# A two-layer attention kernel's set-up: a table load, the small weight products and the slot clearing change places

## The reference

```
xn = layernorm(x)
s  = softmax(q k^T / sqrt(8) + bias[t - s]) v @ w_out + b_out    # 16 heads of 8
g  = silu(sum over the 2 best of 8 experts: weight * expert(xn))
x  = x + s * g
xn = layernorm(x)
s  = (resid * causal_softmax + skip * I - centre * uniform) v @ cproj_w
g  = silu(xn @ W^T + b + (xn @ V_r) @ C^T)
x  = x + s * g
```

## Time and profile before

| what | us |
| --- | --- |
| median of three runs | 993.75 |
| profiled execution | 994.62 |
| its span, first to last instruction | 992.4 |
| TensorE busy | 844.7 (85%) |
| VectorE busy | 726.2 (73%) |
| ScalarE busy | 454.1 (46%) |
| GpSimd busy | 348.1 (35%) |
| start of the first pass of batch 0 | 53.43 |
| start of VectorE's step 1 | 96.68 |

### The profile page before, as it was taken

The page is one execution under the profiler, slowest core; times in us unless marked ns, Lnnn a source line. Parts: engine busy times, 40 slices in busy tenths (PEclk is TensorE's granted clock), DMA queues, the critical chain, the costliest instruction groups (busy, mean ns, idle before and its releaser), DMA issues.

```text
span 992.4 us, 21521 instructions
## 1 busy us (share of the span) xinstructions
PE 844.7 (85%) x7798; PEld 545.6 (55%) x7813; DVE 726.2 (73%) x1155; ACT 454.1 (46%) x803; POOL 348.1 (35%) x369
## 2 busy tenths in 40 slices
PE   1896999999999999887999995255799899999986
PEld 0563555555555555443666663144566676777763
DVE  7638899999998899985767774753377676776753
ACT  1523455444455454443444443582445445454532
POOL 7001755553111111000444444731233433535332
PEclk9987999999999999997999998577799999999998
DMA  5795444444222223231222223304435345354410
GB/s 141 245 191 103 101 98 102 102 108 100 66 64 64 65 64 80 50 120 35 68 65 66 67 69 92 110 17 97 80 87 115 82 101 107 86 116 90 106 28 11
DMA packets 105540, 88.37 MB, mean 89 GB/s; under 512 B 12565, under 2 KB 97497, under 8 KB 102409
## 3 DMA queue, kind: packets, MB, share of 16 engines
q1 hardware_dynamic: 96780, 76.54, 33.8%
q0 software_dynamic: 4352, 8.99, 3.2%
q10 hardware_dynamic: 4352, 2.10, 0.9%
HBM read 45.69 MB, written 41.11 MB: 87 GB/s over the span
## 4 chain that ended last, share of the span: by engine, by line
PE 20%; issue 14%; POOL 8%; DMA 6%; ACT 3%; DVE 2%; SPq 1%; POOLq 0%; ACTq 0%; DVEq 0%
PE ps L751 7%; POOL probs L1221 5%; DMA ks<-parts_d 3%; PE ps L772 3%; PE ps L763 2%; POOL qkr L1208 2%; POOL qk L1213 2%; ACT rows L967 1%; PE ps L753 1%; DMA parts_d<-qk 1%; PE ps L745 1%; PE ps L1487 1%; PE ps L1555 1%; PE ps L1547 1%; DMA probs<-mixed 1%
## 5 line engine op out<-in xcount | busy, mean ns | idle before, releaser
L1269 DVE TENSOR_REDUCE mx<-ps 128x4 f32<-128x1024 f32 (+1 forms) x224 | 270.1, 1219 | 109.6 <-PE ps L1487 75.2
L1410 ACT ACTIVATE probs<-probs 128x1024 f32<-128x1024 f32 x128 | 135.2, 1057 | 149.0 <-DVE probs L1279 146.5
L1279 DVE TENSOR_TENSOR probs<-ps,tabB 128x1024 f32<-128x1024 f32 x128 | 152.7, 1215 | 1.6 <-PE ps L1507 1.6
L1415 ACT ACTIVATE probs<-ps 128x1024 f32<-128x1024 f32 x96 | 96.5, 1023 | 96.7 <-PE ps L1547 38.8
L1538 PE MATMUL ps<-probs,vpad 128*32 128x256 f32 (+1 forms) x2048 | 128.9, 358 | 2.5 <-ACT probs L1410 0.6
L1221 POOL TENSOR_TENSOR probs<-probs 128x512 f32<-128x512 f32 x64 | 78.9, 1264 | 136.3 <-PE ps L1538 136.3
L1479 PE MATMUL ps<-tabA,eyeb 128*128 128x512 bf16 x256 | 100.8, 394 | 20.7 <-DVE probs L1279 14.6
L839 POOL DMA_INDIRECT mixed<-probs x72 | 69.0, 958 | 110.9 <-DVE probs L828 110.3
L1481 PE MATMUL ps<-ks,qs 96*128 96x256 bf16 x512 | 100.7, 278 | 0.0
L1208 POOL TENSOR_TENSOR qkr<-qkf,qk 128x512 f32<-128x512 f32 x32 | 37.0, 1157 | 134.6 <-ACT qk L1382 134.6
L1289 DVE RECIPROCAL rden<-ps 128x256 f32<-128x256 f32 x32 | 56.2, 1756 | 37.0 <-PE ps L1547 25.3
(11 more groups left out here) (228 smaller groups left out, 1578.1 us busy)
## 6 DMA issues: line engine op xcount, KB each, us to landing
parts_d<-qk SPq DMA_DIRECT2D x64, 192.0 KB, 2.2
qs<-parts_d SPq DMA_DIRECT2D x32, 384.0 KB, 4.8
ks<-parts_d SPq DMA_DIRECT2D x32, 384.0 KB, 6.7
parts_d<-qk SPq DMA_DIRECT2D x64, 128.0 KB, 1.9
slots_in<-cum SPq DMA_DIRECT2D x1, 4680.0 KB, 30.6
probs<-slots_in SPq DMA_DIRECT2D x72, 65.0 KB, 1.8
parts_d<-qk SPq DMA_DIRECT2D x64, 64.0 KB, 1.6
probs<-mixed SPq DMA_DIRECT2D x16, 256.0 KB, 3.4
```

The source lines that it names most:

```text
L1269: nc.vector.tensor_reduce(mx[:, s.buf(), t, heads[0]:heads[-1] + 1], ring[:, slot].rearrange("p (h n) -> p h n", n=w), AX.X, ALU.max).then ...
L1279: nc.vector.tensor_tensor(probs[:, j, :].rearrange("p (h n) -> p h n", n=T), ring[:, slot].rearrange("p (h n) -> p h n", n=T), v.tabB[:, h ...
L1410: nc.scalar.activation(probs[:, j, :], probs[:, j, :], ACT.Exp).then_inc(exp_done, 1)
L1415: nc.scalar.activation(probs[:, j, :], ring[:, slot], ACT.Exp).then_inc(exp_done, 1)
```

## The change

Four pieces of the set-up change places.

`tabB` is requested behind `first_stacks()` and no longer right behind `tabA`. On SP:

```diff
-        for i, src in enumerate((v.bias_r, v.bias_f)):
-            sp.dma_start((v.tabA, v.tabB)[i][:], bass.AP(src, 1, [[1, P], [REL, H], [1, TAB]])).then_inc(tab_ld[i], 16)
+        def table(i, of):
+            sp.dma_start((v.tabA, v.tabB)[i][:], bass.AP(of, 1, [[1, P], [REL, H], [1, TAB]])).then_inc(tab_ld[i], 16)
+        table(0, v.bias_r)
         sp.wait_ge(zeroed, ZEROED)
         first_stacks()
+        table(1, v.bias_f)
         ...
-        sp.wait_ge(eb_parts, 1)
-        sp.dma_start(v.slots_in[:, :].rearrange("(t p) d -> p t d", p=P),
-                     v.zero.unsqueeze(1).broadcast_to([P, SLOT_TILES, D + 2])).then_inc(cleared, 16)
         sp.wait_ge(c_load, 16 * 3)
         sp.dma_start(v.share, ...).then_inc(cleared, 16)
```

```diff
+    zeros = v.squares.rearrange("p t d -> p (t d)")[:, 0:SLOT_TILES * (D + 2) // PIECES]
+    def sync_clear(sp):
+        sp.wait_ge(blank, 1)
+        sp.dma_start(v.slots_in[:, :].rearrange("(p k t) d -> p k (t d)", p=P, k=PIECES),
+                     zeros.unsqueeze(1).broadcast_to([P, PIECES, SLOT_TILES * (D + 2) // PIECES])).then_inc(cleared, 16)
+    def gpsimd_clear(pool):
+        pool.wait_ge(ln, layernorm_ready(4) - 2)
+        nc.gpsimd.memset(zeros, 0.0).then_inc(blank, 1)
 ...
                 if s.has(1):
                     stacks(s)
+                if layer == 0 and s.k == 0:
+                    v.sync_clear(sp)
                 if s.has():
                     maxima(s)
 ...
                 body(first)
+                v.gpsimd_clear(pool)
 ...
                     dve.wait_ge(v.eb_stored, 16)
+                    dve.wait_ge(v.cleared_slots, 32)
```

```diff
+        pe.wait_ge(copied, EARLY + 5)
+        for k in range(3, 6):
+            nc.tensor.matmul(ps[:, 2, k:k + 1], rowsp[:, k, :], v.ones[0:1, 0:1], start=True, stop=True)
+        pe.wait_ge(small_cp, 2)
+        nc.tensor.matmul(ps[0:RANK, 2, 128:256], fv, eye, start=True, stop=True)
+        nc.tensor.matmul(ps[0:RANK, 2, 256:384], fc, eye, start=True, stop=True).then_inc(small_mm, 1)
         pe.wait_ge(tab_ld[0], 16)
         pe.wait_ge(bias_cp, 2)
         for n in range(NB):
+            if n == NB // 2:
+                pe.wait_ge(small_cp, 7)
+                nc.tensor.matmul(ps[:, 2, 0:P], bvb, v.wo0[:], start=True, stop=False)
+                ...
+                nc.tensor.matmul(ps[:, 2, P:2 * P], fvT, fcT, start=False, stop=True).then_inc(small_mm, 1)
```

More of the change, by code:

```diff
@@ L166, in build @@
         v.cum = sb("cum", [P, T])
-        v.zero = v.cum[:, 0:D + 2]
         v.yt = sb("yt", [P, T])
@@ L261, in setup @@
     sorted_in, labelled = sem("su_sorted_in"), sem("su_labelled")
+    blank = sem("su_blank")
+    PIECES = 6
+    zeros = v.squares.rearrange("p t d -> p (t d)")[:, 0:SLOT_TILES * (D + 2) // PIECES]
     ZEROED = 13
@@ L383, in sync @@
         sp.dma_start(braw[5 * E:BIASES, :], v.f_b.rearrange("(a n) -> a n", a=1)).then_inc(eb_load, 16)
-        sp.wait_ge(eb_parts, 1)
-        sp.dma_start(v.slots_in[:, :].rearrange("(t p) d -> p t d", p=P),
-                     v.zero.unsqueeze(1).broadcast_to([P, SLOT_TILES, D + 2])).then_inc(cleared, 16)
         sp.wait_ge(c_load, 16 * 3)
         sp.dma_start(v.share, v.consts[0, C_UT:C_UT + T].partition_broadcast(P)).then_inc(cleared, 16)
+    def sync_clear(sp):
+        sp.wait_ge(blank, 1)
+        sp.dma_start(v.slots_in[:, :].rearrange("(p k t) d -> p k (t d)", p=P, k=PIECES),
+                     zeros.unsqueeze(1).broadcast_to([P, PIECES, SLOT_TILES * (D + 2) // PIECES])).then_inc(cleared, 16)
     def sync_late(sp):
-        sp.wait_ge(eb_parts, 6)
+        sp.wait_ge(eb_parts, 5)
         sp.dma_start(v.bias3_d[:].rearrange("c r n -> r c n"), b3[:]).then_inc(eb_stored, 16)
@@ L426, in vector @@
         nc.vector.memset(v.eps[:], EPS).then_inc(ln, 1)
-        nc.vector.memset(v.zero, 0.0).then_inc(eb_parts, 1)
         nc.vector.memset(v.ones[:], 1.0).then_inc(copied, 1)
@@ L464, in vector @@
                               gains[0:1, 0, :].unsqueeze(2).broadcast_to([1, H, HD])).then_inc(copied, 1)
+        dve.wait_ge(small_mm, 2)
+        nc.vector.tensor_scalar(v.cols[:, 3:4], ps[:, 2, 3:4], QSCALE, None, ALU.mult).then_inc(small_cp, 1)
+        nc.vector.tensor_copy(v.cols[:, 4:6], ps[:, 2, 4:6]).then_inc(small_cp, 1)
+        nc.vector.tensor_copy(fvT, ps[0:RANK, 2, 128:256]).then_inc(small_cp, 1)
+        nc.vector.tensor_copy(fcT, ps[0:RANK, 2, 256:384]).then_inc(small_cp, 1)
         layernorm_scale(nc, dve, v, ln, sq, rs, 1)
@@ L474, in vector @@
         nc.vector.tensor_copy(v.maskB[:], cst[:, C_MB:C_MB + P]).then_inc(copied, 1)
[L475 to L479, removed]
         dve.wait_ge(small_mm, 3)
@@ L489, in vector_late @@
             if c < PARTS - 1:
+                dve.wait_ge(eb_parts, 2 * c + 1)
+                nc.vector.tensor_tensor(braw[:], braw[:], b3[:, c, :], ALU.subtract).then_inc(eb_parts, 1)
                 dve.wait_ge(eb_parts, 2 * c + 2)
-                nc.vector.tensor_tensor(braw[:], braw[:], b3[:, c, :], ALU.subtract).then_inc(eb_parts, 1)
-                dve.wait_ge(eb_parts, 2 * c + 3)
         routing(dve)
@@ L575, in tensor @@
         for n in range(NB):
+            if n == NB // 2:
+                pe.wait_ge(small_cp, 7)
+                nc.tensor.matmul(ps[:, 2, 0:P], bvb, v.wo0[:], start=True, stop=False)
+                nc.tensor.matmul(ps[:, 2, 0:P], v.ones[0:1, 0:P], bor, start=False, stop=True)
+                nc.tensor.matmul(ps[:, 2, P:2 * P], fw, eye, start=True, stop=False)
+                nc.tensor.matmul(ps[:, 2, P:2 * P], fvT, fcT, start=False, stop=True).then_inc(small_mm, 1)
             if n >= 3:
@@ L585, in tensor @@
         pe.wait_ge(copied, EARLY + 10)
[L586 to L595, removed]
         pe.wait_ge(tab_cp, NB)
@@ L624, in setup @@
     v.unit_cp, v.sorted_in, v.eb_stored = unit_cp, sorted_in, eb_stored
+    v.gpsimd_clear, v.sync_clear, v.cleared_slots = gpsimd_clear, sync_clear, cleared
     v.scatter, v.sync_late, v.vector_late, v.scalar_late, v.tensor_late = scatter, sync_late, vector_late, scalar_late, tensor_late
```

## The result

The changed kernel took 984.87 us, median of four runs (984.37 to 988.03), the kernel before 992.98 beside it (four runs, 991.84 to 995.19): a ratio of 0.9922, 95% interval 0.9894 to 0.995. The forecast was 989.0 in a range of 985.4 to 993.4. The profiled run took 988.03 us with a span of 985.9, against 994.62 and 992.4 before: 6.5 us of span.

The account below looks back on a forecast made before the run. TensorE was taken to set the pace from the first pass, itself released by batch 0's late `ks`; 3.4 (first pass) + 1.4 (clock) + 0 (clearing) = 4.8 us off the median 993.75 gave 989.0, range 985.4 to 993.4.

Parts of the forecast that it names:

- the stacks: SP's queue: with `tabB` behind them, batch 0's stacks land at 45.9 instead of 53.3, 7.4 us earlier.
- what covers the rest: Set-up: `tabB` landing near 54.3 and VectorE's second normalisation, 2.2 us later, stay hidden behind TensorE's work, costing nothing.
- the small products and F: TensorE before the first pass: products moved ahead, first pass starts at 50.0 instead of 53.43, gaining 3.4 us (1.9 to 5.5).
- the plain sum: TensorE from 36.53: flips, transposes, scores and small products one after the other without waits, ending at 50.5.
- The clock's term: TensorE's first pass: fewer waits shorten the low-clock stretch, gaining 1.4 us, the middle between none and 2.9.
- The rival in which the clock holds: TensorE: products at 2.4 GHz, first pass near 48.8 at high clock, 7.5 us gain, 986.3 us; chance 0.20.
- the clearing: SP's queue behind batch 1's stacks: 16 us of flow, landing at 84 before VectorE's step 1 needs it, cost nothing.
- The rival of a late clearing: VectorE's step 1 waits if the clearing flows over 28.7 us; at 50.8 us the time is 1016; chance 0.08.
- The memset: GpSimd at 42 to 43.5: zeroing takes some 1.3 us and could delay VectorE's second normalisation by up to 1.3.

Follow-up runs that it names:

- e2: Only the nine small products and VectorE's four copies moved, against the kernel before; table and clearing as before: 991.75 us, ratio 0.9997.
- e5: The changed kernel again without edit, 12 runs, against the kernel before: 986.75 us, ratio 0.9949.
- e10: The changed kernel again without edit, 6 runs, against the kernel before: 985.87 us, ratio 0.9932.
- e4: The changed kernel with the clearing back in its old place and rows of 520 bytes: 989.52 us, ratio 0.9979 to the kernel before.
- e6: The changed kernel with the late clearing in 9216 rows of 520 bytes instead of 768 pieces: 989.86 us, ratio 0.9977 to the kernel before.
- e9: The changed kernel with three of `tabB`'s flip units moved from the first pass to behind A7: 979.8 us, ratio 0.9873 to the kernel before.
- e3: Only the clearing moved late, in 6240-byte pieces with GpSimd's memset, against the kernel before: 991.41 us, ratio 1.0001.
- e8: The changed kernel with unread TensorE products about flips and scores, plus 25 from 14.5 to 28 us and up to the first transposes: 986.29 us, ratio 0.9955.
- e11: The kernel before once more, no edit, one run: 987.26 us.

## Why the prediction was right in its mechanism and too small in its size

**Right: the stacks.** Forecast 45.9, landed near 46.0, set by the parts and no longer by `tabB`. e1, which moves the table alone, has the same 9.2 us from the parts (35.88) to the landing; e2 shows the reverse: without this part F stays at 53.26.

**Right: what covers the rest.** `tabB` was put at 54.3 and came at 55.5, hidden. VectorE's reduction was put at 39.5 and came at 39.75, hidden. VectorE showed no idle time ahead of V, and the gain of 6.0 there is 6.2 at step 2's division and 6.5 at the span's end.

**Too small: the small products and F.** This is the step that failed. It added up 14.0 us of TensorE's work from 36.53, took 0.5 off for ScalarE's overlap, left the last four products at their time at 1.2 GHz, and chose F = 50.0 "near the plain sum" of 50.5. F was 48.51, a gain of 4.9 us where 3.4 was taken (4.2 and 5.2 in e5 and e10; its bounds were 1.9 to 5.5). The rows split the 2.0 us below the plain sum. In the kernel before, the transposes behind the flips start at 42.64:

```profile
42.64 0.60 PE L560 MATMUL ps<-cst,rows 128*128 128x128 f32 x4
```

So the twelve flips took 42.64 - 36.53 = 6.1 us there. In the changed kernel's trace the first flip has no matmul record (eleven of twelve are listed), but its weight load starts at 39.1. The first six flips thus took 41.78 - 39.1 = 2.7 us and the other six 45.86 - 43.58 = 2.3, together 1.1 less than before. Some 0.5 of this was not in the prediction at all: ScalarE's first copy came 37.67 - 36.53 = 1.1 us behind the first flip, held up by ScalarE's earlier work, and now comes 39.75 - 39.1 = 0.6 behind it. The other 0.6 is the overlap, near the forecast of 0.5: ScalarE's copies pause for 44.01 - (39.75 + 3.04) = 1.2 us while TensorE spends 1.8 on the four products. The largest part is the clock of these four: 43.58 - 41.78 = 1.8 us where they took 3.0. The prediction had priced this (up to 2.6 us for both groups) and then put it at nothing. Against these stand the first five, which took 39.1 - 36.74 = 2.4 us for 2.2 and began 0.2 late; transposes and scores took 0.1 less. The sum is -1.1 - 1.2 - 0.1 + 0.2 + 0.2 = -2.0. The rows of the kernel before could not tell whether the four would run fast: in four of the nine traces with the products moved they did not.

**The clock's term: right in size.** 1.4 us forecast, 2.9 - 1.7 = 1.2 in the profiled run and as much in e10; about 0.5 in e5, where it was low until 54. The middle of 0 and 2.9 was a choice between two bounds, so that it came so close is luck. The rival in which the clock holds came true in part: the last four products ran at 2.4 GHz and F lies near its 48.8, but the first five did not, and the first pass did not stay at the high clock. That its time, 986.3, is nearer the three medians than the forecast is luck too. The rule from the Trainium skill, TensorE: Matmul & The Clock Gate, Part 1, that activity releases the low clock, agrees with the rise near 52.5; the fall ahead of it, with TensorE busy 1.66 us of 2 and then all of 2, was not in what I drew from it.

**Right in sign, wrong in size: the clearing.** It was put at 16 us of flow between 12.8 and 25.4; behind batch 1's `ks`, 59.95 + 6.7 = 66.7, it took 78.4 - 66.7 = 11.7, less than the lower bound, at 409 to 424 GB/s. It cost nothing, as forecast. What the prediction did not see is what its removal from the early place is for: it named the 23.16 us of held-up SP, but not that with F earlier this would be the next wait. e4 shows it: 5.71 us at step 1. The rival of a late clearing needed a flow of over 28.7 us; e6 shows that with the old rows its neighbours on the queue do get late, for 1.66 us.

**The memset.** 1.40 us for a forecast of 1.3, at 42.07 (42). The Trainium skill, SBUF — State Buffer, section SBUF: two separate sides, limits the lock to certain VectorE operations. Here the reciprocal ran from 43.01 to 43.26 within the memset, which ended at 42.07 + 1.40 = 43.47, and the product behind it took its 2.29 us. No run shows this memset holding VectorE.

**The base and the range.** The forecast's ratio, 989.0 / 993.75 = 0.9952, lies within the intervals of e5 and e10 and just above that of the four runs shown first. The range was built from the edit's terms alone around a median of three; yet one and the same kernel before ran from 986.24 to 996.4 in 35 runs. So the range's low end, 985.4, had to hold a larger F and a spread that the text knew only from three runs. The step above does not by itself carry the time out of the range. Of the 4.1 us from 989.0 to 984.87, 1.7 are the profiled span's gain of 6.5 instead of 4.8, with 1.5 from F, -0.2 from the clock and the rest behind V; 0.8 are the base, 992.98 beside the changed kernel instead of 993.75; and 1.6 are the medians' 8.1 instead of the span's 6.5, which no row explains. The medians gained 4.2 us in e5 and 6.9 in e10, and the times of both lie inside the range. How much of the difference between 8.1 and 4.2 is chance can't be said beyond the intervals.

## What to carry over

When a wait is removed, work out the engine's own sum behind it with each group at both clock levels and with the copies that run beside it, since that sum is the new time, and a term that hangs on the clock needs both its bounds in the range. Then ask what the same queue holds up next, for here three edits of which two gave nothing alone made one gain. Where the engine that sets the pace is itself idle a few microseconds later, moving work there (e9) was worth 6 us by the medians, near the 6.9 of the whole change in the same set. A base from three runs is not known to better than its spread, and a range has to hold that too.

## What the runs showed of the hardware beyond what was expected

- A load's issue can hold its engine long behind a store of many rows: the 128 KB load of the share took 23.16 to 26.47 us to issue behind 9216 rows of 520 bytes, and 0.35 us without them. A 16 KB load of biases took 6.4 to 7.6 us to issue right behind `tabB`'s load (the changed kernel, e1 and e4 to e10), and 0.42 where that load had landed before (the kernel before, e2 and e3). Behind 768 pieces of 6240 bytes a small store took 0.93 us, behind the rows 9.33.
- The same 4680 KB flowed at 409 to 424 GB/s in long pieces with a DMA share of 1.0, landing 18.0 us behind the issue; in rows they landed 30.0 us behind it (e6).
- One program's clock differs from run to run: low in about 3.4 us of the first pass in two traces of the changed kernel, in 4.7 in the third, with F from 48.19 to 49.24. Windows that print a granted clock of 1.00 held the same three products (line 585) at 1.44 us in the changed kernel's trace and at 0.82 in e5's. Over the 35 runs of the kernel before beside e1 to e4 and the 35 beside e5 to e8, a run's mean granted clock (0.934 to 0.952) and its time correlate at -0.71 and -0.57, over the 11 beside e9 to e11 at -0.36.
